# Expert routing moved into the attention loop by groups of four chunks, with a token list in DRAM (attention plus mixture of experts, one core)

## The chip, the cores and the metric

The kernel runs on one core of a Trainium2 chip. Times are device microseconds (us) of one execution. The engines of the core are PE (matrix multiply), DVE (vector), ACT (scalar), POOL (GpSimd) and SP, which here only issues transfers. Each engine works through its own list of instructions strictly in the order in which they are written, and waits on semaphores for the others. PE's clock has two levels, 1.2 and 2.4 GHz; the profile shows the granted one as 0.5 and 1.00.

## The reference, cut to what matters

```python
# x: (4, 1024, 256), 4096 tokens, 8 experts, 16 heads, chunks of 128 tokens
xn = _layernorm(x)
# attention: causal linear attention with phi(q), phi(k), then y @ w_proj.T
gate_logits = einsum('bsd,ed->bse', xn, gate_w) + gate_b + expert_bias
top_idx = argmax(gate_logits, axis=-1)
for e in range(8):
    mask = (top_idx == e)[..., None]
    h = relu(einsum('bsd,df->bsf', xn, w1[e]) + b1[e])
    y = einsum('bsf,fd->bsd', h, w2[e]) + b2[e]
    out = out + mask * y
x = x + attention(xn) + out
```

Each token goes to one expert only. The kernel sorts the tokens by expert, so that each expert's matrices meet only its own tokens.

## The kernel before

The program has two stages. The **attention loop** runs over `p` from 0 to 36. There are NC = 32 chunks of 128 tokens (`c`), and each engine works in iteration `p` on several chunks at different steps. On PE, iteration `p` holds `scores` and `st` of chunk p-3, `ktr` of p-2, `xt` of p-1 (the transpose of the normalised input, L324), `mx` in every fourth iteration, `yt1` of p-4, `inter` of p-3, `mxa` in every fourth iteration, `qk` of p-1 (L341), `yt2`, `vg` of p-1 (L355, values and gate logits), `pr` and `pv`. Nothing reorders the work: the order of the calls in each engine's loop is the order of its queue.

POOL feeds PE in this loop. In each iteration it runs, in this order: `nn` (the inverse square root of the variances, 14 dependent small instructions, in every even `p`), `km` (L1092, masks q for two heads; PE's `scores` wait for it), `w_lo` (L1101, the low half of a quarter of expert weights), `xl` (L1085, the low half of the normalised input) and a second `w_lo`. PE's `xt(c)` waits for `xl(c)`. DVE's `nb` (L606, the normalised input) waits for `nn`, and ACT's `xh` (L941) for `nb`; `xl` waits for `xh`.

DVE runs `phi` (L657), two `s_mask` (L663), `y`, two more `s_mask`, `t32`, in every fourth iteration `scale` (L720 to L724, whose result PE's `vg` waits for), `nb`, `w_max` (L698), `sums`, `res` (L691), `na`, and a second `w_max`. ACT copies results out of PSUM and makes the high halves (`w_hi`, L997).

**Routing before** comes at the end. `pick` (L754 to L768) chooses the experts of chunks 0 to 30 in one go in iteration 32, and of chunk 31 in iteration 33. `counts` on PE (L458, L460), then `bases` and `ranks` on DVE find each token's place in the sorted order. After the loop DVE builds comparison tables (L853, L856) and PE multiplies them (L519), which gives `ids`: for each of NS = 39 slots of 128 tokens the row number of each token. Then the **expert stage** gathers 128 rows of `scr` for a slot (an indirect transfer from POOL, L1136), transposes them (L528), runs the two matrices of the slot's expert (L550, L564) and scatters the result to the output (L1141).

Of the kernel before, what the change touches and what calls it, by code (L numbers as in the profile page):

```python
# [14 lines left out]
NT = B * T  # L15
# [3 lines left out]
E = 8  # L19
# [10 lines left out]
C_ID, C_MASK, C_ME, C_MH, C_ONE, C_WT, C_SL, C_T, C_N = (0, 128, 256, 258, 266, 274, 282, 321, 322)  # L30

D_RST, D_P, D_ID, D_N = (0, 264, 392, 424)
# [27 lines left out]
def program(nc, x, wall, wp, gb, eb, w1, b1, w2, b2, cst, cst2, tri, out):  # L60
    ctx = ExitStack()
    with ctx:
# [15 lines left out]
        L = sb("L", [128, NC, E], F32)  # L78
        GBE = sb("GBE", [128, 2, E], F32)
# [62 lines left out]
        PMA = PS[1][:, 392:394]  # L142
        PBX = PS[7][0:8, 0:128]
# [4 lines left out]

        VA = ST[:, 0:2048]
        R1 = VA[:, 0:256].rearrange("p (c e) -> p c e", e=E)  # L150
        R2 = VA[:, 256:512].rearrange("p (c e) -> p c e", e=E)
        O32 = VA[:, 512:768].rearrange("p (c e) -> p c e", e=E)

        TT = VA[:, 768:1032].rearrange("p (e c) -> p e c", e=E)
        PI = VA[:, 1032:1296].rearrange("p (e c) -> p e c", e=E)
        M1 = VA[:, 1296:1328]
        M2 = VA[:, 1328:1360]
        SLI = VA[:, 1360:1392].bitcast(I32)
        PLI = VA[:, 1392:1424].bitcast(I32)
        POSI = VA[:, 1424:1456].bitcast(I32)  # L160
        NSI = VA[:, 1456:1464].bitcast(I32)
        NSF = VA[:, 1464:1472]
        CSF = VA[:, 1472:1480]
        BAS = VA[:, 1480:1488]
        O16 = VA[:, 1488:1616].bitcast(BF16)
        O16C = O16.rearrange("p (c e) -> p c e", e=E)
        LC = VA[:, 1624:2048]
        EQS = VA[:, 0:624].bitcast(F16).rearrange("p (c s) -> p c s", c=32)
        WAF = WA[:, :, :, :].rearrange("p l k n -> p (l k n)")
        BO = WAF[:, 0:1248].rearrange("p (c s) -> p c s", c=32)  # L170
        GE = WAF[:, 1248:1248 + 14 * NS].bitcast(F32).rearrange("p (s e) -> p s e", e=7)
        ESF, IDZ, IDP = (WAF[:, o:o + 2 * NS].bitcast(F32) for o in (1800, 1880, 1960))
        AO = [t[:, :].bitcast(F16).rearrange("p (c n) -> p c n", c=8) for t in XR[0:4]]
# [14 lines left out]
        scr = nc.dram_tensor("scr", [NT, 512], F32, kind="Internal").ap()  # L188
        outr = out.rearrange("b t d -> (b t) d")
# [27 lines left out]

        def experts(engine, tile, unit, s):
# [10 lines left out]
        d_wall, d_wp, d_cst, d_tri, d_small, d_cst2, d_b2 = (  # L229
            sem(n) for n in ("d_wall", "d_wp", "d_cst", "d_tri", "d_small", "d_cst2", "d_b2"))  # L230
# [9 lines left out]
        names = ("sums", "na", "nn", "nb", "xh", "xl", "xt", "xTc", "qk", "relu", "exp", "phi", "km", "sc", "pv", "ktr", "kt",  # L240
# [8 lines left out]
        v_o16, t_cnt, v_es, v_bo, v_ao, t_ids, v_ids, p_xg0 = (  # L249
            sem(n) for n in ("v_o16", "t_cnt", "v_es", "v_bo", "v_ao", "t_ids", "v_ids", "p_xg0"))  # L250
# [7 lines left out]
        def sync(e):  # L258
# [27 lines left out]
            e.dma_start(WPF, wp).then_inc(d_wp, 16)  # L286
            for c in range(4, R):
                load_x(c)
            for n in range(4):
                load_split(n)  # L290
            for p in range(NC + 5):
# [12 lines left out]
                if p == NC:  # L304
                    e.wait_ge(v_wmx, NW)
                    e.dma_start(LC, cst2).then_inc(d_cst2, 16)
            e.dma_start(B2, b2).then_inc(d_b2, 16)

        def tensor(e):
# [35 lines left out]
            def vg(c):  # L345
                if c >= 1:
                    e.wait_ge(S["lg"], c)
                    e.wait_ge(S["vh"], c)
                if (c + 1) // 4 >= 1:
                    e.wait_ge(v_sc, 3 * ((c + 1) // 4))  # L350
                n = 0
# [856 lines left out]
```

## Time and profile before

| | |
|---|---|
| median of 3 runs | 545.98 us (545.52 to 548.12) |
| the profiled execution | 550.78 us |
| its span, first to last instruction | 549.0 us |
| attention loop | to about 294 us |
| routing, first gathers | 294 to 312 us |
| expert stage | 312 us to the end |
| PE busy | 484.5 us (88%) |
| DVE, ACT, POOL busy | 405.8, 280.1, 287.8 us |

The profiled execution is 0.9% longer than the median; a difference found in it is carried over to the median as it is. In a row of a timeline the first number is the start in us from the span's start, the second the duration; a bracket at its end gives the idle time before it and what ended it. Several instructions of one kind can be merged in one row (x24).

### The profile page before, as it was taken

What the parts mean: (1) busy time and instruction counts of PE and PEld (TensorE: products, weight loads), DVE (VectorE), ACT (ScalarE), POOL (GpSimd) and SP (SyncE); (2) the same over time, 40 slices, a digit from 0 to 9 for tenths busy, and PEclk for the clock granted to TensorE, in tenths of its full rate; (3) what the DMA queues carried; (4) which work ended last, traced back from release to release, by engine and by line L of the source; (5) the groups of instructions that cost most, each with busy time, mean ns of one, the idle gap of its engine ahead of it and who ended that gap; (6) DMA issues with size and microseconds to landing.
All of it is one profiled execution on the core that took longest, in us unless ns stands there. A gap on an engine that the chain in (4) does not pass through costs nothing.

```text
span 549.0 us, 17451 instructions
## 1 busy us (share of the span) xinstructions
PE 484.5 (88%) x6065; PEld 394.8 (72%) x6065; DVE 405.8 (74%) x869; ACT 280.1 (51%) x535; POOL 287.8 (52%) x480
## 2 busy tenths in 40 slices
PE   4499999999999999999862499899989989989991
PEld 1378888788878888888741388688868868868871
DVE  2768898888988898888777477677757667676671
ACT  0446878878787878878652033233323333333330
POOL 3645788777777877777434323433432433433321
PEclk9579999999999999999995599999999999999997
DMA  8322655665566556653332212222121221120100
GB/s 283 120 79 70 211 156 193 184 206 182 163 194 192 177 164 213 199 151 132 116 113 100 76 31 69 60 64 79 55 62 59 70 73 59 60 78 22 32 6 0
DMA packets 34016, 62.44 MB, mean 114 GB/s; under 512 B 5517, under 2 KB 9998, under 8 KB 33808
## 3 DMA queue, kind: packets, MB, share of 16 engines
q1 hardware_dynamic: 28944, 48.74, 28.4%
q0 software_dynamic: 4992, 12.60, 7.7%
q8 instruction: 55, 0.90, 0.6%
q14 instruction: 25, 0.20, 0.1%
HBM read 50.57 MB, written 13.50 MB: 117 GB/s over the span
## 4 chain that ended last, share of the span: by engine, by line
PE 80%; DVE 10%; issue 5%; ACT 2%; DMA 1%; POOL 1%; DVEq 0%; POOLq 0%; ACTq 0%
PE ps L550 20%; PE ps L564 19%; PE ps L341 6%; PE ps L379 6%; PE ps L408 6%; PE ps L449 6%; PE ps L355 4%; PE ps L392 3%; PE ps L422 2%; DVE AR L663 2%; PE ps L435 2%; PE ps L528 2%; PE ps L362 1%; PE ps L441 1%; PE ps L314 1%
## 5 line engine op out<-in xcount | busy, mean ns | idle before, releaser
L550 PEld LDWEIGHTS ps<-AR,W 128*128 x1872 | 131.7, 99 | 39.9 <-issue 1.0
L564 PE MATMUL ps<-W,ST 128*128 x624 | 150.8, 326 | 7.0 <-DVE AR L918 3.7
L550 PE MATMUL ps<-AR,W 128*128 128x128 f16 x1872 | 155.8, 221 | 0.8 <-ACT AR L1034 0.8
L1141 POOL DMA_INDIRECT out<-AR x39 | 39.6, 1016 | 130.0 <-DVE AR L918 130.0
L886 DVE SCALAR_TENSOR_TENSOR ST<-ps,TAs,B1S 128x512 f32<-128x512 f32 x78 | 58.5, 750 | 57.6 <-PE ps L550 56.9
L1043 ACT ACTIVATE ST<-ST 128x512 f16<-128x512 f32 x78 | 49.3, 631 | 99.9 <-DVE ST L886 96.4
L663 DVE TENSOR_TENSOR AR<-ps,CT 128x512 f32<-128x512 f32 x128 | 82.1, 684 | 12.1 <-PE ps L379 11.6
L1101 POOL TENSOR_TENSOR W<-ST,W 128x512 f16<-128x512 f32 x64 | 74.5, 1165 | 26.6 <-ACT W L997 26.2
L1092 POOL TENSOR_SCALAR AR<-AR,CT 128x256 f32<-128x256 f32 x64 | 58.7, 927 | 15.2 <-DVE AR L657 15.2
L898 DVE SCALAR_TENSOR_TENSOR ST<-ST 128x512 f16<-128x512 f32 x78 | 53.8, 690 | 15.7 <-ACT ST L1043 15.7
L1136 POOL DMA_INDIRECT AR<-scr,AR x39 | 45.4, 1165 | 28.6 <-issue 11.0
L1034 ACT ACTIVATE AR<-ps 128x512 f16<-128x512 f16 x39 | 23.3, 597 | 68.9 <-PE ps L528 68.6
L341 PE MATMUL ps<-xT,WA 128*128 128x128 f16 x768 | 50.7, 225 | 3.9 <-ACT xT L947 3.9
L564 PEld LDWEIGHTS ps<-W,ST 128*128 128x128 f16 x624 | 45.6, 98 | 10.0 <-issue 7.7
L341 PEld LDWEIGHTS ps<-xT,WA 128*128 128x128 f16 x768 | 46.7, 101 | 5.5 <-ACT xT L947 5.2
L1005 ACT ACTIVATE ST<-ST,SC 128x512 f32<-128x512 f32 x64 | 46.4, 725 | 0.0
L698 DVE TENSOR_REDUCE MX<-ST 128x1 f32<-128x512 f32 x64 | 42.5, 665 | 0.0
L997 ACT ACTIVATE W<-ST 128x512 f16<-128x512 f32 x64 | 40.4, 632 | 1.1
L379 PE MATMUL ps<-AR 32*128 32x256 f32 x512 | 37.4, 407 | 0.0
L1085 POOL TENSOR_TENSOR XR<-AR,XR 128x256 f16<-128x256 f32 x32 | 22.9, 714 | 27.3 <-ACT XR L941 27.2
L449 PE MATMUL ps<-AR 128*128 128x256 f32 x128 | 35.5, 401 | 1.4 <-ACT AR L990 1.4
L408 PE MATMUL ps<-AR 128*32 128x128 f32 x1024 | 34.6, 276 | 0.0
(144 smaller groups left out, 756.2 us busy)
## 6 DMA issues: line engine op xcount, KB each, us to landing
ST<-in_w SPq DMA_DIRECT2D x128, 256.0 KB, 4.3
scr<-XR SPq DMA_DIRECT2D x32, 256.0 KB, 2.1
XR<-in_x SPq DMA_DIRECT2D x32, 128.0 KB, 4.7
AR<-in_b SPq DMA_DIRECT2D x1, 1024.0 KB, 4.9
AR<-in_wall SPq DMA_DIRECT2D x1, 776.0 KB, 4.5
AR<-scr,AR POOLq DMA_INDIRECT x39, 3.5
out<-AR POOLq DMA_INDIRECT x39
AR<-in_wp SPq DMA_DIRECT2D x1, 256.0 KB, 4.8
```

Source lines behind the costliest of these rows:

```text
L341: a = e.matmul(PS[0][:, j * 128:(j + 1) * 128], WA[:, wl, k, j * 128:(j + 1) * 128], x_part(c, xl_, k), start=(n == 1), stop=(n == 6))
L379: a = e.matmul(PSC[r][:, g * 256:(g + 1) * 256], QK[c % 2][rows, 256 + g * 128:384 + g * 128], QM[c % 2][rows, g], start=True, stop=True)
L408: a = e.matmul(PS[5][32 * b:32 * b + 32, j * 128:(j + 1) * 128], V32[c % 2][:, 8 * g + 4 * i + b, :], S32[2 * i + t][:, (2 * g + o) * 128: ...
L449: a = e.matmul(PS[2][:, 256:512], YT2[:, k * 128:(k + 1) * 128], WPF[:, k, :], start=(k == 0), stop=(k == 1))
L550: a = e.matmul(dst, W[:, off:off + 57472][:, bass.ds(at[s], 128)], XT16[s % 2][:, xl * 256 + k * 128:xl * 256 + (k + 1) * 128], start=(n = ...
L564: a = e.matmul(PS[4 + s % 2][:, 0:w], src[h % 4][:, fs], W[:, off:off + 57344 + w][:, bass.ds(at[s], w)], start=(f == 0 and w == 512), sto ...
L663: e.tensor_tensor(S32[r].rearrange("p (b n) -> p b n", b=4), PSC[r][:, :].rearrange("p (b n) -> p b n", b=4), msk, ALU.mult).then_inc(s_[r ...
L886: e.scalar_tensor_tensor(H32[h % 2].rearrange("p (f n) -> p f n", f=4), PS[h % 4][:, :].rearrange("p (f n) -> p f n", f=4), TAs[:, :, 0][: ...
L898: e.scalar_tensor_tensor(HL2[h % 4], H32[h % 2], 0.0, HH[h % 4], ALU.max, ALU.subtract).then_inc(v_hl, 1)
L1043: e.activation(HH[h % 4], H32[h % 2], ACT.Relu).then_inc(a_hh, 1)
L1092: a = e.tensor_scalar(QM[c % 2][:, :, o, :], QK[c % 2][:, 0:256].rearrange("p (g n) -> p g n", g=2), cc(C_ME + o, 1), None, ALU.mult)
L1101: e.tensor_tensor(lo_, src, hi, ALU.subtract).then_inc(p_wlo, 1)
```

## The change

The choice of experts, the ranks and the places in the list are worked out for four chunks at a time inside the attention loop. With g as the number of the group:

- `pick` (DVE, p = 5 + 4g) takes the four chunks' logits and now has 6 instructions of 128x32 elements; the two biases are added up once beforehand.
- `ahead` (POOL, p = 5 + 4g): four dependent additions of 128x8 elements that count the tokens of the chunks ahead.
- `place` (PE, p = 6 + 4g): three matmuls of 32 columns give each token its rank within its expert plus 4096 times the expert. `own` (DVE, two small instructions) selects it, `rows` (POOL) converts it to integers.
- `put` (POOL, one for each chunk, from p = 6 on; the last four all in iteration 34): an indirect transfer that writes 128 token numbers of 4 bytes each to their places in the list `lst` in DRAM. `lst` is filled with an out-of-range number at the start.
- `slots` (DVE, p = 34) works out which 39 rows of the list hold tokens. One indirect transfer on POOL reads these 39 rows of 128 numbers into `TOK`, PE transposes them, and DVE copies them to `ids`.
- The comparison tables, their 32 matmuls and a constant's load in the loop are gone.

Beside this: POOL's `km` is halved, ACT makes the other half (`km`, after `xTc`). ACT runs `xh` and the second `w_hi` after `relu` and `exp` instead of before. On DVE `scale` moves from behind the last two `s_mask` and `t32` to behind `y`. POOL clears the gather buffers in iteration 35, ahead of the last four `w_lo`, instead of behind them.

```diff
+            def place(p):
+                g = group(p, 6)
...
+                e.wait_ge(v_o16, g + 1)
+                e.wait_ge(p_ox, g + 1)
...
+                e.matmul(PRK, tri16[:, :], O16[:, g % 2], start=True, stop=False)
+                e.matmul(PRK, one16[:, :], OX[:, g % 2], start=False, stop=False)
+                a = e.matmul(PRK, one16[0:1, :], B4[:, :, :], start=False, stop=True)
...
+            def pick(p):
+                g = group(p, 5)
...
+                e.tensor_tensor(R1[:, :, :], l, bm(GBE[:, 2, :], 4), ALU.add).then_inc(dv.up(), 1)
...
+                e.tensor_tensor(o, bc(M1[:, :], E), w, ALU.is_equal).then_inc(v_o16, 1)
...
+                own(p)
                 if on(p - 4):
                     y(p - 4)
+                scale(p)
                 if on(p - 3):
                     s_mask(p - 3, 2)
                     s_mask(p - 3, 3)
                     t32(p - 3)
-                scale(p)
                 if on(p) and p > 0:
                     nb(p)
                 w_max(2 * p)
+                pick(p)
...
-            e.tensor_tensor(BO, EQS, bc(LC[:, D_ID:D_ID + 32], NS), ALU.mult).then_inc(v_bo, 1)
-            for g in range(4):
-                e.wait_ge(d_scr[g], 16 * (NC // R))
-                e.tensor_tensor(AO[g], bm(LC[:, D_P:D_P + 128], 8), bc(M2[:, 8 * g:8 * g + 8], 128),
-                                ALU.is_equal).then_inc(v_ao, 1)
...
+            def ahead(p):
...
+                e.wait_ge(v_o16, g + 1)
...
+                for i in range(4):
+                    dst = OX[:, g % 2, i + 1] if i < 3 else OX[:, (g + 1) % 2, 0]
+                    a = e.tensor_tensor(dst, OX[:, g % 2, i], O16[:, g % 2, i], ALU.add)
...
+            def put(c):
...
+                e.indirect_dma_start(lst, bass.IndirectOffsetOnAxis(POS[:, c % 4:c % 4 + 1], 0),
+                                     cc(C_TK + c, 1), None, bounds_check=E * NT - 1,
+                                     oob_is_err=False).then_inc(d_put[c % 4], 16)
...
                 if on(p - 2):
-                    km(p - 2)
+                    km2(p - 2)
+                ahead(p)
+                rows(p)
+                if p < NC + 2:
+                    if on(p - 6):
+                        put(p - 6)
+                elif p == NC + 2:
+                    for c in range(NC - 4, NC):
+                        put(c)
+                if p == NC + 3:
+                    e.wait_ge(S["pv"], NC)
+                    for i in range(NG):
+                        e.memset(XG[i], 0.0).then_inc(p_xg0, 1)
                 w_lo(2 * (p - 5))
                 if on(p):
                     xl(p)
                 w_lo(2 * (p - 5) + 1)
+                if p == NC + 2:
+                    e.wait_ge(v_row, 1)
+                    for i in range(4):
+                        e.wait_ge(d_put[i], 16 * (NC // 4))
+                    e.indirect_dma_start(TOK, None, lst.rearrange("(r n) o -> r (n o)", n=128),
+                                         bass.IndirectOffsetOnAxis(ROI[0:NS, :], 0), bounds_check=E * NT // 128 - 1,
+                                         oob_is_err=False).then_inc(d_tok, 16)
```

The queue of POOL in an iteration p = 9 (a second group's `pick`) and the start of the next, before: one masking pair (L1092), `w_lo`, `xl`, `w_lo`, then `nn` of p = 10.

```order
L1092 TENSOR_SCALAR AR<-AR,CT 128x2x128 [waits s_sc,s_phi]
L1092 TENSOR_SCALAR AR<-AR,CT 128x2x128
L1101 TENSOR_TENSOR W<-ST,W 128x512 [waits a_whi]
L1085 TENSOR_TENSOR XR<-AR,XR 128x256 [waits s_xh]
L1101 TENSOR_TENSOR W<-ST,W 128x512 [waits a_whi]
L1063 TENSOR_SCALAR rsn<-mv 128x2 [waits s_nb,s_na]
```

The same place after. L1106 is the half of the masking that is left, L1119 `ahead`, L1141 a `put`, L1150 `w_lo`, L1100 `xl`.

```order
L1106 TENSOR_SCALAR AR<-AR,CT 128x2x128 [waits s_sc,s_phi]
L1119 TENSOR_TENSOR OX<-OX,O 128x8 [waits t_rk,v_o16]
L1119 TENSOR_TENSOR OX<-OX,O 128x8 [waits po] x3
L1141 DMA lst<-CT,POS 32768x1
L1150 TENSOR_TENSOR W<-ST,W 128x512 [waits a_whi]
L1100 TENSOR_TENSOR XR<-AR,XR 128x256 [waits s_xh]
L1150 TENSOR_TENSOR W<-ST,W 128x512 [waits a_whi]
L1078 TENSOR_SCALAR rsn<-mv 128x2 [waits s_nb,s_na]
```

One masking instruction has gone; four additions that wait for DVE's `pick` (v_o16) and one indirect transfer now stand ahead of `w_lo` and `xl`.

DVE in such an iteration after, from the end of `pick` on (L775 to L788), with `sums` (L609), `res` (L710) and `phi` (L676) behind it:

```order
L775 TENSOR_TENSOR R<-L,GBE 128x32 [waits s_lg]
L777 TENSOR_REDUCE M<-R 128x4 [waits dv]
L779 TENSOR_TENSOR R<-R,M 128x32 [waits dv]
L781 TENSOR_TENSOR R<-R,CT 128x32 [waits dv]
L783 TENSOR_REDUCE M<-R 128x4 [waits dv]
L788 TENSOR_TENSOR O<-M,CT 128x32 [waits dv]
L609 BN_STATS st<-XR 128x6 [waits s_na,d_x3]
L710 TENSOR_TENSOR XR<-ps,XR 128x256 [waits s_pr]
L616 BN_AGGR mv<-st 128x2 [waits s_nn,s_sums]
L717 TENSOR_REDUCE MX<-ST 128x1 [waits d_wm3]
L676 SCALAR_TENSOR_TENSOR AR<-ps,AR 128x512 [waits s_exp]
```

Before, `sums` followed the first `w_max` at once; now six dependent instructions stand between them.

POOL at the end of the attention loop before, the last four iterations' `w_lo` (L1101), the clearing of the gather buffers (L1126) and the first gathers (L1136):

```order
L1101 TENSOR_TENSOR W<-ST,W 128x512 [waits a_whi] x4
L1101 TENSOR_TENSOR W<-ST,W 128x2x256 [waits a_whi] x4
L1126 MEMSET AR 128x512 [waits s_pv]
L1126 MEMSET AR 128x512 x3
```

And after, from the last `ahead` to the first gather (L1205); L1134 is `rows`, L1192 the reading of the list:

```order
L1119 TENSOR_TENSOR OX<-OX,O 128x8 [waits po] x3
L1141 DMA lst<-CT,POS 32768x1
L1150 TENSOR_TENSOR W<-ST,W 128x512 [waits a_whi] x2
L1134 CAST POS<-M 128x4 [waits d_put2,d_put1,d_put3,d_put0,v_pos]
L1141 DMA lst<-CT,POS 32768x1 [waits p_pos]
L1141 DMA lst<-CT,POS 32768x1 x3
L1150 TENSOR_TENSOR W<-ST,W 128x512 [waits a_whi] x2
L1192 DMA ST<-lst,ST 39x128 [waits d_put2,d_put1,d_put3,d_put0,v_row]
L1183 MEMSET AR 128x512 [waits s_pv]
L1183 MEMSET AR 128x512 x3
L1150 TENSOR_TENSOR W<-ST,W 128x2x256 [waits a_whi] x4
L1205 DMA AR<-scr,AR 128x512 [waits d_scr4,d_scr5,d_scr3,d_scr6,d_scr2,d_scr7,d_scr1,v_ids,d_scr0,p_xg0]
```

Six indirect transfers now stand in POOL's queue between the last `ahead` and the first gather.

## Rows read from the trace of the kernel before

**Rows 1.** Engines' busy time by stretches: columns PE, PEld, DVE, ACT, POOL, clock, DMA

```profile
166.00:197.50 31.50, 31.25 (x431) 26.69 (x427) 27.34 (x66) 25.43 (x53) 24.48 (x49) 1.00 0.58 183
...
294.00:312.00 18.00, 2.38 (x36) 1.67 (x36) 13.25 (x30) 0.33 (x2) 6.79 (x10) 0.50 0.31 102
```

**Rows 2.** Timeline of PE, xt of two chunks, and PE's wait for scale

```profile
183.12 0.39 PE L324 MATMUL ps<-id,XR 128*128 128x128 f16 x4
...
190.82 0.39 PE L324 MATMUL ps<-id,XR 128*128 128x128 f16 x4
...
PE ps L355 <- DVE SC L724: 1.9, 7, 0.3
```

**Rows 3.** Timeline of DVE, sums in an iteration p = 4n + 1; nb's durations

```profile
179.59 0.42 DVE L593 BATCH_NORM_STATS2 st<-XR 128x6 f32<-128x256 f32 x1
...
L606 DVE TENSOR_SCALAR AR<-XR,mv,rsn x32: 404/408/1424, 15.1 to 257.2; 128x256 f32<-128x256 f32 x32
```

**Rows 4.** Timeline of DVE: pick of 31 chunks and of one

```profile
267.81 0.41 DVE L754 TENSOR_TENSOR ST<-L,GBE 128x248 f32<-128x248 f32 x1
268.25 0.42 DVE L756 TENSOR_TENSOR ST<-ST,GBE 128x248 f32<-128x248 f32 x1
...
277.68 0.16 DVE L754 TENSOR_TENSOR ST<-L,GBE 128x8 f32<-128x8 f32 x1
277.87 0.17 DVE L756 TENSOR_TENSOR ST<-ST,GBE 128x8 f32<-128x8 f32 x1
```

**Rows 5.** Timeline of POOL, iteration p = 4n + 2 from nn on

```profile
181.49 0.22 POOL L1063 TENSOR_SCALAR rsn<-mv 128x2 f32<-128x2 f32 x1
...
184.85 0.19 POOL L1074 TENSOR_SCALAR nr<-nr 128x2 f32<-128x2 f32 x1
185.13 0.20 POOL L1076 TENSOR_TENSOR rsn<-rsn,nr 128x2 f32<-128x2 f32 x1
185.30 1.84 POOL L1092 TENSOR_SCALAR AR<-AR,CT 128x256 f32<-128x256 f32 x2
187.11 1.16 POOL L1101 TENSOR_TENSOR W<-ST,W 128x512 f16<-128x512 f32 x1
188.23 0.67 POOL L1085 TENSOR_TENSOR XR<-AR,XR 128x256 f16<-128x256 f32 x1
188.86 1.16 POOL L1101 TENSOR_TENSOR W<-ST,W 128x512 f16<-128x512 f32 x1
```

**Rows 6.** Gathers by line (ns, least/median/most; idle us, times), then the last scatter's chain

```profile
L1136 POOL DMA_INDIRECT AR<-scr,AR x39: 997/1029/1548, 307.5 to 518.9; - x39
  issue: 11.0, 36
...
539.19 0.73 issue
539.92 0.98 POOL out L1141
```

**Rows 7.** Timeline of PE at the end of attention, and the clock behind

```profile
271.88 0.53 PE L362 MATMUL ps<-CT,AR 128*128 128x128 f32 x2 [1.72 <-DVE AR L657]
...
284.88 0.28 PE L458 MATMUL ps<-ST,tri 128*128 128x256 bf16 x1
285.00 0.27 PE L460 MATMUL ps<-ST,one 128*128 128x256 bf16 x1
...
272.00:274.00 2.00, 1.88 (x9) 1.58 (x10) 1.34 (x4) 1.52 (x4) 2.00 (x3) 0.52 0.00 0
```

**Rows 8.** Timeline of DVE and POOL between the stages

```profile
271.15 0.68 DVE L657 SCALAR_TENSOR_TENSOR AR<-ps,AR 128x512 f32<-128x512 f32 x1
...
300.51 4.62 DVE L856 TENSOR_TENSOR XR<-ST 128x1024 f16<-128x1024 f32 x4
...
295.40 1.95 POOL L1126 MEMSET AR<- 128x512 f32 x4
...
307.53 1.27 POOL L1136 DMA_INDIRECT AR<-scr,AR  x1 [10.18 <-DVE AR L867]
```

More of the change, by code:

```diff
@@ L149, in program @@
         VA = ST[:, 0:2048]
[L150 to L173, printed above, removed]
+        NSI = VA[:, 0:8].bitcast(I32)
+        NSF, CSF, DOF, GEP = (VA[:, 8 * i:8 * i + 8] for i in range(1, 5))
+        ROW = VA[:, 40:41]
+        ROI = VA[:, 41:42].bitcast(I32)
+        ESF = VA[:, 64:64 + NS]
+        GE = VA[:, 128:128 + 7 * NS].rearrange("p (s e) -> p s e", e=7)
+        TOK = VA[0:NS, 512:640]
         wt = cc(C_WT, 8)
@@ L188, in program @@
         scr = nc.dram_tensor("scr", [NT, 512], F32, kind="Internal").ap()
+        lst = nc.dram_tensor("lst", [E * NT, 1], F32, kind="Internal").ap()
         outr = out.rearrange("b t d -> (b t) d")
@@ L216, in weights, with group @@
             return src.rearrange("p (f n) -> p f n", f=2), w[:, :, 0], w[:, :, 1]
+        def group(p, first):
+            g = (p - first) // 4
+            return g if (p - first) % 4 == 0 and 0 <= g < NC // 4 else None
         def experts(engine, tile, unit, s):
@@ L350, in vg @@
                     e.wait_ge(v_sc, 3 * ((c + 1) // 4))
+                if group(c + 1, 6) is not None:
+                    e.wait_ge(v_pos, group(c + 1, 6) + 1)
                 n = 0
@@ L490, in tensor @@
                 mx(p)
+                place(p)
                 if p == 2:
@@ new lines, in pick, with own @@
+                e.tensor_tensor(o, bc(M1[:, :], E), w, ALU.is_equal).then_inc(v_o16, 1)
+            def own(p):
+                g = group(p, 6)
+                if g is None:
+                    return
+                e.wait_ge(t_rk, g + 1)
+                e.tensor_tensor(R1[:, :, :], PRK, O16[:, g % 2], ALU.mult).then_inc(dv.up(), 1)
+                e.wait_ge(dv.sem, dv.n)
+                if g >= 1:
+                    e.wait_ge(p_pos, g)
+                e.tensor_reduce(M2[:, :], R1[:, :, :], X_AX, ALU.add).then_inc(v_pos, 1)
@@ L966, in kt, with km @@
                 e.activation(KT32[c % 2], PS[0][:, 0:256], ACT.Copy).then_inc(S["kt"], 1)
+            def km(c):
+                e.wait_ge(S["phi"], c + 1)
+                if c >= 2:
+                    e.wait_ge(S["sc"], c - 1)
+                e.activation(QM[c % 2][:, :, 0, :], QK[c % 2][:, 0:256].rearrange("p (g n) -> p g n", g=2),
+                             ACT.Copy, scale=cc(C_ME, 1)).then_inc(S["km"], 1)
             def vh(c):
@@ L977, in lg @@
             def lg(c):
-                e.activation(L[:, c, :], PS[1][:, 256:264], ACT.Copy, scale=sv(1)).then_inc(S["lg"], 1)
+                if c >= 8:
+                    e.wait_ge(v_o16, c // 4 - 1)
+                e.activation(L[:, c // 4 % 2, c % 4, :], PS[1][:, 256:264], ACT.Copy, scale=sv(1)).then_inc(S["lg"], 1)
             def y1(c):
```

226 lines of the change are left out of this document (115 added, 111 removed).

## The prediction

> **What bounds the kernel now.** I read the busy time by stretches first. In four iterations of the attention loop PE is busy for 31.25 of 31.50 us, while DVE has 4.1 us free and POOL 7.0 us, some of it only short gaps between dependent instructions [rows 1]. PE sets the pace: one `xt` follows the other after 7.70 us [rows 2]. The one thing that PE waits for regularly is DVE's `scale`, 1.9 us in 7 waits [rows 2]. Between 294 and 312 us PE has 2.38 us of work and waits for the routing at half clock [rows 1]. So there are two accounts: what the change saves at the seam of the stages, and what it puts in the way of a PE that has no slack in the loop. In the loop nothing PE does can be late for free, so the question for each added step is only whether it reaches PE.
>
> **Account 1, the seam.** Before, the first gather is at 307.53 [rows 8]. What stands before it and goes: `pick` of 31 chunks holds DVE from 267.81 to 271.15, 3.34 us, and the next `phi` with it, for which PE waits 1.72 us [rows 4, 7, 8]; the tables, of which the last four instructions alone take 4.62 us [rows 8]. What will stand there instead is POOL's queue; I follow it in the time frame of before, without the delays from account 2.
> - The last `pick`: that of one chunk started at 277.68 [rows 4]. Without the 3.34 us, and since `pick` now stands ahead of `res`, which costs it about 1.1 us less waiting (an estimate from the order alone), it starts at 273.2.
> - Its six instructions are of 32 elements. Start to start it is 0.19 us at 8 elements and 0.44 at 248 [rows 4]; at 32 that is 0.22, so 1.35 us for six. POOL sees it 0.1 us later.
> - `ahead`: dependent small instructions on POOL follow at 0.28 us [rows 5]: 3 x 0.28 + 0.20 = 1.05 us. To 275.7.
> - An indirect transfer holds POOL for 1.03 us, plus 11.0/36 = 0.31 us ahead of it in a stream [rows 6]: **1.31 us**. With the gap of an isolated one, 0.73 us, it is 1.73 us [rows 6]. The trace has no transfer of 4-byte elements; these two are my bounds. It has the same 128 addresses as a gather, and compute instructions stand ahead of it that let POOL prepare, so I take the lower.
> - From 275.7: one `put` 1.31, two `w_lo` at 1.16 [rows 5], `rows` 0.3 (one small instruction and a wait), four `put` 5.25, two `w_lo`, the reading of the list 1.31, clearing 1.95 [rows 8], four `w_lo` 4.64. That gives 295.1, and the first gather some 0.3 us later, 295.4. The gain is **12.1 us**; with 1.73 us for each of the six transfers and 0.73 at the gather it is 9.2.
> - What could bind later than POOL: the list lands some 3 us after 288.5, is transposed and copied by about 292.5; the last rows of `scr` are written by about 292. Both are before 295.
>
> **Account 2, the loop.** `scale` moves ahead of two `s_mask`: PE's 1.9 us of waits go (**-1.9**). `place` adds three matmuls with their own weights; the two of this kind before were issued 0.12 us apart [rows 7], so 0.3 us for each group and all of it on PE, since PE has no gap. ACT's half of `km` and the later `xh` I cost at nothing: ACT has 6 us free in 31.5 [rows 1], and POOL's `xl`, which waits for `xh`, has to be ready more than a us later than `xh` will be in the iterations without `pick`.
>
> The expensive part is the order on POOL. `ahead` waits for `pick` of the same iteration, and `put`, `w_lo` and `xl(p)` stand behind it; PE's `xt(p)` waits for that `xl`. The iteration around 180 us is one in which `pick` will be:
> - `pick` can start where `sums` starts now, at 179.59 [rows 3]. DVE is there tied to PE's progress through `y`, so it can't come earlier.
> - From there: pick 1.35, semaphore 0.1, `ahead` 1.05, `put` 1.31, `w_lo` 1.12, `xl` 0.67 [rows 4 to 6], 5.6 us. `xl` is ready at 185.2. PE wants it at 183.12 [rows 2]. PE waits **2.1 us** (2.5 with the dearer transfer).
> - The next iteration starts from that late `xl`. POOL runs `w_lo` to `nn`'s start 1.2 us, `nn` 3.81 (181.49 to 185.30), half of `km` 0.92, `rows` 0.3, `put` 1.31, `w_lo` 1.12, `xl` 0.67 [rows 5, 6]: 9.35 us from one `xl` to the next. PE needs 7.70 + 0.3 = 8.0 us from one `xt` to the next. PE waits another **1.35 us** (1.8).
> - In the third iteration there is no `nn` and POOL catches up (5.2 us of work for 7.7). In the fourth `nn` is back, but it starts early enough: from the second `xl` on, two iterations of work come to 14.7 us against 15.9 on PE. Then POOL idles until the next `pick`. So the delay does not grow, and it comes back in each group.
>
> For each group 2.1 + 1.35 + 0.3 = 3.75 us (4.65 with the dearer transfer). Groups 1 to 6 have all of it, 22.5 us (27.9). Group 0 has no `put` yet in its first iteration, 0.8 + 1.35 + 0.3 = 2.45 us (3.0). Group 7 lies in account 1. At the start POOL gets two more small instructions ahead of the second `xl`, 0.4 us.
>
> **The sum**: -12.1 - 1.9 + 22.5 + 2.45 + 0.4 = **+11.4 us**; with the dearer transfer -9.2 - 1.9 + 27.9 + 3.0 + 0.4 = +20.2 us. Against the profiled execution's 550.78 us this is 562.2; against the median of 545.98, 0.9% lower, it is **557.4 us**, 2.1% slower.
>
> **POOL and DVE sharing a path.** `nb` took 408 ns at the median and 1424 ns once [rows 3], and one gather took 1548 ns where most took 1029 [rows 6]: now and then an instruction of one of the two waits for the other. If each of the 13 `put` on PE's path met such a case, 0.5 us each, the sum would be 6.5 us more. I don't count it, since 1 in 39 gathers can hardly be told from the median. The Trainium skill, SBUF — State Buffer, sections SBUF: two separate sides and Who interferes with whom, says that a DVE instruction in a two-port mode takes the path shared with GpSimd for its whole length and that the other blocks, and it names descriptor writing as a victim. By that rule a `put` would wait for at most one `nb`. The trace agrees only in part: `nb` mostly ran at 408 ns beside a busy POOL.
>
> **The rivals.**
> - *A `put` hardly holds POOL* (the engine goes on while the descriptors are written). This one ends faster. With 0.3 us instead of 1.31, the two waits fall to 1.1 and 0.35 us, a group to 1.75: 10.5 + 1.45 - 1.9 + 0.4 = +10.5 in the loop. The seam then is bound by the list and the last `scr` rows at about 293, gain 14.5. Sum -4, **542 us**. Against it: the gathers stand 1.3 us apart with nothing else in the queue. For it: POOL's spans are rough, and the gathers show the spacing of transfers alone, not that of a compute instruction behind one. Each 0.1 us of a `put` is worth 1.9 us (13 in the loop, 6 at the seam), so the sign turns at 0.7 us. Chance 0.15.
> - *The late `xl` does not reach PE*, because DVE gets ahead of its present place after the first wait, or `pick` is quicker. Then -12.1 - 1.9 + 2.1 + 0.4 = -11.5, **534.5 us**. Against it: `y` waits for `yt1` of the same iteration, and the distance from there to `pick` is a sum of DVE durations. Chance 0.07.
> - *Half of it*: cheaper transfers and one of the two waits. 543 to 549 us, chance 0.12.
> - *PE's clock falls in the waits.* After 1.72 us of waiting PE's granted clock was 0.52 from 272 to 274 us [rows 7]; the waits forecast here are 2.1 us long and come seven times. At half clock PE falls back by about 1.7 us each time, but the second wait of a group, for POOL, takes up 1.35 of that. So it adds 0.4 to 1.7 us a group, and with the dearer transfer this gives 564 to 573 us. Chance 0.16.
> - The forecast: 551 to 564 us, chance 0.50.
>
> **How the numbers follow.** A measurement of this kernel can tell about 0.5% (2.7 us) from no change. Faster by more: the first two rivals, which give 0.22. Within 0.5%: most of the third, 0.10. Slower: 0.68. The range for 8 in 10 leaves out the second rival, part of the first and the dearest ends of the fourth: 540 to 569 us. The likeliest case by itself has 551 to 564.
>
> **What would show it.** In the profile after: POOL's four additions wait for DVE's `pick` in every fourth iteration, some 4 us in all; PE's transposes (L331) have a wait of about 2 us for POOL's `xl` (L1100) in one iteration and 1 to 1.5 us in the next, six times each; four iterations take 35 us where they took 31.5. The waits for `scale` are gone. The first gather comes 12 us after the place it would have in a loop without delays, so near 319 us, and the expert stage is as long as before. The prediction is wrong if a `put` holds POOL for less than 0.7 us, if `pick` starts earlier relative to PE's `yt1`, or if the clock falls in most groups.

## The result, and the profile after

The changed kernel takes **578.17 us** (576.65 to 579.97, 4 runs) against 545.86 us (545.52 to 548.12, 4 runs) on the same chip, a ratio of 1.058 (95% interval 1.054 to 1.063). Slower was forecast; the size was not: 557.4 us, with 569 as the upper end. The runs of the kernel before fall into two groups, 545.4 to 546.6 and 548.0 to 551.2 us, whose mix changes from one set of runs to the next (its median by sets: 545.9 to 549.3), so two ratios from different sets can differ by up to 0.6% for that alone. The traces show where in the program such a difference can arise: PE's clock is at half level until 33 us in the profiled execution of before, and only in part of that stretch in the one of e4, whose loop is as long.

```profile
20.00:33.00 13.00, 11.31 (x81) 9.24 (x85) 7.28 (x18) 5.90 (x13) 7.08 (x23) 0.50 0.40 122
...
20.00:33.00 13.00, 10.60 (x118) 8.70 (x116) 9.47 (x23) 6.30 (x15) 7.72 (x20) 0.85 0.35 107
```

The first row is of before, the second of e4. The sixth `xt` stands at 56.87 us in the one and at 52.27 in the other; in after it stands at 57.35.

The profiled execution of after took 579.97 us, 17.8 us more than the 562.2 that the prediction's sum gives for the profiled execution. The rows below say where these 17.8 us are. Busy time by stretches, with the columns of [rows 1]:

```profile
166.00:202.00 36.00, 31.67 (x426) 26.30 (x425) 29.32 (x75) 26.60 (x58) 26.21 (x54) 1.00 0.69 165
...
294.00:338.00 44.00, 18.15 (x199) 12.69 (x196) 18.06 (x55) 16.03 (x30) 23.07 (x29) 0.73 0.47 95
```

PE now has 4.3 us free in four iterations of 36 us, where it had 0.25 in 31.5 [rows 1]. Its clock is at 1.00 in this stretch. The share of DMA has risen from 0.58 to 0.69, though the rate fell from 183 to 165 GB/s: the transfers have become longer, not more. The waits from 60 to 300 us (engine, line, waited for; sum, times, longest):

```profile
POOL OX L1119 <- DVE O L788: 27.3, 6, 4.8
...
PE ps L331 <- POOL XR L1100: 15.5, 11, 2.1
...
DVE AR L622 <- POOL rsn L1091: 9.5, 7, 1.7
...
PE ps L389 <- DVE XR L710: 6.9, 14, 0.8
...
ACT ST L1017 <- DMA ST<-in_w: 2.3, 5, 0.7
```

The first two rows are the forecast: `ahead` waits for `pick`, and PE's `xt` for `xl`. The other three were not forecast: DVE's `nb` (L622) waits for POOL's `nn`, PE's `scores` (L389) for DVE's `res` (L710), and ACT's scaling of weights for their load. In PE's timeline the waits for `xl` and for `res` stand in each group; here are the second iteration of one and the first two of the next:

```profile
208.06 1.15 PE L389 MATMUL ps<-AR 32*128 32x256 f32 x16 [0.77 <-DVE XR L710]
...
210.85 0.40 PE L331 MATMUL ps<-id,XR 128*128 128x128 f16 x4 [0.76 <-POOL XR L1100]
...
233.14 1.15 PE L389 MATMUL ps<-AR 32*128 32x256 f32 x16 [0.37 <-DVE XR L710]
...
236.86 0.40 PE L331 MATMUL ps<-id,XR 128*128 128x128 f16 x4 [2.12 <-POOL XR L1100]
...
243.84 1.15 PE L389 MATMUL ps<-AR 32*128 32x256 f32 x16 [0.77 <-DVE XR L710]
...
246.63 0.40 PE L331 MATMUL ps<-id,XR 128*128 128x128 f16 x4 [0.76 <-POOL XR L1100]
...
252.57 1.15 PE L389 MATMUL ps<-AR 32*128 32x256 f32 x16 [0.17 <-DVE XR L710]
```

`xt` waits 2.12 us in one iteration (forecast 2.1; 1.70 in some groups) and 0.76 in the next (forecast 1.35); the 0.77 for `scores` ahead of it makes up the rest and 0.18 more. The waits of 0.37 and 0.17 for `res` stand beside the forecast ones. POOL in the first of these iterations:

```profile
232.41 1.03 POOL L1119 TENSOR_TENSOR OX<-OX,O 128x8 bf16<-128x8 bf16 x4 [4.36 <-DVE O L788]
233.95 1.04 POOL L1141 DMA_INDIRECT lst<-CT,POS  x1 [0.50 <-issue]
235.02 1.16 POOL L1150 TENSOR_TENSOR W<-ST,W 128x512 f16<-128x512 f32 x1
236.14 0.67 POOL L1100 TENSOR_TENSOR XR<-AR,XR 128x256 f16<-128x256 f32 x1
```

A `put` holds POOL for 1.04 us. Ahead of it stand 0.50 us behind `ahead`, 0.3 in a stream, and 0.78 behind `rows`, whose result it waits for: 1.3 to 1.8 us, where 1.31 was taken and 1.73 was the upper bound. So the price of the step that was in doubt was nearly right, a little low behind `rows`. Now POOL at the seam, from the last `ahead` to the first gather:

```profile
302.90 1.04 POOL L1119 TENSOR_TENSOR OX<-OX,O 128x8 bf16<-128x8 bf16 x4 [4.60 <-DVE O L788]
304.45 1.04 POOL L1141 DMA_INDIRECT lst<-CT,POS  x1 [0.51 <-issue]
305.52 2.28 POOL L1150 TENSOR_TENSOR W<-ST,W 128x512 f16<-128x512 f32 x2
309.28 0.19 POOL L1134 CAST POS<-M 128x4 int32<-128x4 f32 x1 [1.48 <-DMA lst<-CT,POS]
310.24 1.00 POOL L1141 DMA_INDIRECT lst<-CT,POS  x1 [0.77 <-POOL POS L1134]
...
314.13 0.98 POOL L1141 DMA_INDIRECT lst<-CT,POS  x1 [0.31 <-issue]
315.12 2.28 POOL L1150 TENSOR_TENSOR W<-ST,W 128x512 f16<-128x512 f32 x2
326.45 1.01 POOL L1192 DMA_INDIRECT ST<-lst,ST  x1 [9.05 <-DMA lst<-CT,POS]
...
333.99 1.06 POOL L1205 DMA_INDIRECT AR<-scr,AR  x1 [0.16 <-issue]
```

Two waits for puts to land, 1.48 and 9.05 us, stand in POOL's queue. The durations between them are close to the forecast ones. How long one put takes from issue to landing:

```profile
DMA to landing us min/median/max: 3.9/6.3/11.4
```

The longest is that of the last one; it stands in the chain that ended last:

```profile
314.13 11.36 DMA lst<-CT,POS
```

**The 17.8 us.** The last instruction of the last `pick` should have started at 273.2 + 5 x 0.22 = 274.3 in the frame without delays, plus 23.5 us of delay in the loop, 297.8; it started at 302.63. The loop thus cost 4.8 us more than forecast, as far as the estimated start of `pick` without delays is right. From there to the first gather the prediction had 21.1 us; it took 31.4, 10.3 more, and the two waits are 10.5. After the last scatter's issue (566.43) the span runs 11.67 us on, before it was 549.0 - 539.92 = 9.08 [rows 6]: 2.6 more. Together 17.7. The expert stage itself, from the first gather to the last scatter, is as long as before: 232.4 us in both. Against the forecast median of 557.4 us the miss is 20.8 us, 3.0 more: the prediction took 4.8 us off its profiled figure to get to the median, and after's profiled execution lies only 1.8 us above its median.

### The profile page after: what moved, and what is told of

Same layout as the page of the kernel before. It is cut to its first block, busy times and chain, and to the rows that moved or that the text cites. A ratio compares the mean times of both kernels' runs of the same rounds, so it can differ in the third digit from the quotient of the medians.

```text
span 578.1 us, 17672 instructions
## 1 busy us (share of the span) xinstructions
PE 487.2 (84%) x6057; PEld 396.6 (69%) x6057; DVE 404.7 (70%) x902; ACT 288.0 (50%) x567; POOL 296.6 (51%) x524
## 4 chain that ended last, share of the span: by engine, by line
PE 62%; POOL 14%; DVE 9%; issue 8%; DMA 4%; ACT 1%; POOLq 0%; DVEq 0%; ACTq 0%
PE ps L566 18%; PE ps L580 18%; PE ps L348 4%; PE ps L389 3%; POOL W L1150 3%; DMA lst<-CT,POS 3%; PE ps L418 3%; PE ps L402 3%; POOL lst L1141 2%; PE ps L459 2%; PE ps L445 2%; PE ps L432 2%; PE ps L364 2%; POOL XR L1100 2%; PE ps L544 2%
## 5 line engine op out<-in xcount | busy, mean ns | idle before, releaser
L1150 POOL TENSOR_TENSOR W<-ST,W 128x512 f16<-128x512 f32 x64 | 74.3, 1165 | 4.2 <-ACT W L1009 3.4
L1205 POOL DMA_INDIRECT AR<-scr,AR x39 | 40.6, 1041 | 19.1 <-issue 11.2
L389 PE MATMUL ps<-AR 32*128 32x256 f32 x512 | 36.8, 399 | 9.1 <-DVE XR L710 7.2
L1141 POOL DMA_INDIRECT lst<-CT,POS x32 | 33.8, 1056 | 13.2 <-issue 6.9
L389 PEld LDWEIGHTS ps<-AR 32*128 32x128 f32 x512 | 24.3, 184 | 16.5 <-issue 16.3
## 6 DMA issues: line engine op xcount, KB each, us to landing
AR<-in_b SPq DMA_DIRECT2D x1, 1024.0 KB, 12.7
```

Source lines behind the costliest of these rows:

```text
L389: a = e.matmul(PSC[r][:, g * 256:(g + 1) * 256], QK[c % 2][rows, 256 + g * 128:384 + g * 128], QM[c % 2][rows, g], start=True, stop=True)
L1150: e.tensor_tensor(lo_, src, hi, ALU.subtract).then_inc(p_wlo, 1)
```

## The experiments

Ratios are to the kernel before on the same chip, with 95% intervals; "after" is 1.058. e2, e3, e5, e6, e7 and e9 do not compute the reference: their list lacks the tokens whose puts are left out or go elsewhere (e3 lacks three chunks, e2, e5, e6 and e7 all but the last four, e9 all), and the expert stage moves no rows for these. In the traces of e2, e5, e6, e7 and e9 that stage takes 231.0 to 231.1 us instead of 232.4, so some 0.3% of their gain is this. "The loop" below is the time from the sixth `xt` to the last: 204.8 us in before, 232.8 in after.

| run | what | ratio | interval |
|---|---|---|---|
| e1 | `ahead` behind `xl` | 1.034 | 1.030 to 1.038 |
| e2 | no puts in the loop | 1.020 | 1.017 to 1.023 |
| e3 | one last put, not four | 1.047 | 1.045 to 1.050 |
| e4 | before, `scale` early | 0.999 | 0.997 to 1.001 |
| e5 | e1 and e2 | 1.011 | 1.007 to 1.015 |
| e6 | e1, puts of 512 bytes | 1.019 | 1.015 to 1.023 |
| e7 | e1, puts 512 bytes apart | 1.019 | 1.015 to 1.024 |
| e8 | before, all side edits | 1.009 | 1.006 to 1.012 |
| e9 | e7, the last four too | 1.002 | 0.999 to 1.004 |
| e10 | a complete list of that kind | 1.006 | 1.004 to 1.009 |
| e11 | e10, `xh` early on ACT | 1.017 | 1.010 to 1.024 |
| e12 | e10, seam reordered | 1.002 | 0.999 to 1.004 |
| e13 | before, side edits without late `xh` | 1.002 | 0.999 to 1.006 |
| e14 | e12, `slots` split | **0.994** | 0.992 to 0.996 |

**The place of `ahead` (e1).**

```diff
-                ahead(p)
                 rows(p)
...
                 if on(p):
                     xl(p)
+                ahead(p)
```

> Changed kernel with one move on POOL: the four additions of ahead stand behind xl instead of ahead of put, w_lo and xl. Nothing else is changed. Theory A (what costs in the loop is that xl stands behind a wait for pick): by the time xl is done pick has ended, so ahead no longer waits long; four iterations fall from 35.8 us to 31.5 to 32.5 us, PE's waits for xl (L1100) nearly go, and the time falls by 20 to 25 us, to 553 to 558 us. Theory B (POOL simply has too much to do with the puts, wherever the wait stands): four iterations stay above 34.5 us, and the time stays above 570 us. The seam between the stages is the same in both.

568.45 us, between the ranges of both theories. The wait of `xt` for `xl` nearly goes, and another comes out (60 to 260 us):

```profile
ACT ST L1017 <- DMA ST<-in_w: 12.3, 5, 3.6
...
PE ps L331 <- POOL XR L1100: 2.7, 4, 0.8
```

The order on POOL is worth 2.4% by the ratios; the medians, from two chips, differ by 9.7 us and the traced spans by 12.7, of which 9.8 are in the loop. What it uncovers are weight loads that land late. A put took 7.3 us to land here, a weight load 5.9 (4.3 before).

**The puts themselves (e2, e5).** The call of `put` in the loop is left out.

> Changed kernel without the 28 indirect transfers of the loop (puts of chunks 0 to 27); the last four stay. The list in DRAM then holds only the last 512 tokens, so most slots gather and scatter nothing. Theory A (the puts are 1.1 to 1.5 us each in the two iterations in which xl is late): each group loses 2.5 to 3 us, four iterations fall to about 33 us and the loop is 15 to 18 us shorter. Theory C (the wait for pick by itself is the cost, the puts hardly matter): four iterations stay above 35 us. The landing of the last put tells something as well: if it stays near 11 us after its issue, earlier puts have no part in it.

560.88 us. The loop takes 218.4 us, 14.4 less than in after, four iterations 33.6: Theory A, roughly. Even without these puts the kernel is 2.0% slower: `ahead` still waits for `pick` ahead of `xl`. And the last put landed 14.3 us after its issue, with POOL's reading of the list waiting behind it:

```profile
311.13 1.00 POOL L1188 DMA_INDIRECT ST<-lst,ST  x1 [11.94 <-DMA lst<-CT,POS]
```

So the puts of the loop have no part in the late landing of the last four. Both edits together:

> Both earlier edits together: ahead stands behind xl, and the loop's 28 puts are left out (the list then holds only the last 512 tokens). Theory F (the loop's excess has two parts, the place of ahead and the puts, and nothing else): four iterations take 31.5 to 32.2 us as in the kernel before, and the weight loads land in 4.3 us. Against e2, whose loop took 33.6 us for four iterations, that is 8 to 12 us less in all: 549 to 553 us where before is 549. Rival: ACT's new half of km, the later xh and place cost PE by themselves, then four iterations stay above 32.7 us.

552.87 us, in the expected range, but with 32.6 us for four iterations (31.5 before, 35.8 after), between what Theory F and its rival expected: the place of `ahead` and the puts are not quite all of the loop's excess.

**Size or address (e6, e7).** Both have e1's order and write the loop's puts into a second tensor. The first added line is of e6, the others are of e7.

```diff
+                dst, val = (lst2, cc(C_ID, 128)) if c < NC - 4 else (lst, cc(C_TK + c, 1))
...
+                e.tensor_scalar(POS[:, :], M2[:, :], 128.0 if g < NC // 4 - 1 else 1.0, None,
+                                ALU.mult).then_inc(p_pos, 1)
```

> As e1 (ahead behind xl), but the loop's 28 puts write 512 bytes for each token into a tensor of 512-byte rows instead of 4 bytes into the list (the list then holds only the last 512 tokens). In e1 a put landed 7.3 us after its issue and the weight loads in 5.9 us. Theory G (writes of a few bytes are slow by themselves and hold the transfer engines): with 128 times the bytes the puts land in 2 to 4 us, as the scatters of the expert stage do, the weight loads are back at 4.2 to 4.6 us, and the time falls to 551 to 556 us. Rival H (any 128 scattered writes from POOL's queue beside the loads do it): landings stay near 7 us and the time near 565 us.

> As e1, but the loop's 28 puts write their 4 bytes at places 512 bytes apart in another tensor (the list then holds only the last 512 tokens). In the list, tokens of one expert stand at neighbouring addresses, so several transfer engines write into the same few bytes' neighbourhood. Theory I (neighbourhood is what makes them slow): the puts land in 2 to 4 us and the weight loads in 4.2 to 4.6 us, as forecast for e6. Theory G (the size alone): as slow as in e1, landing near 7 us, weight loads near 5.9 us, time 565 to 569 us.

558.26 and 559.10 us, both 1.5% below e1, of which 0.3% is the shorter expert stage. The landings are as Theories G and I have them, the times are above their 551 to 556 us. The queue's issues in e7 (KB each, median us to landing), which in after read 5.1, 3.2 and 6.3:

```profile
ST<-in_w SPq DMA_DIRECT2D x128, 256.0 KB, 4.1
scr<-XR SPq DMA_DIRECT2D x32, 256.0 KB, 2.2
...
lst<-CT,POS POOLq DMA_INDIRECT x32, 3.7
```

Words of 4 bytes that lie 512 bytes apart land as fast as rows of 512 bytes (3.7 us in both), those next to each other take twice that (7.3 in e1). So it is the neighbouring address and not the small size; that it isn't the second tensor either, e10 shows below. The Trainium skill, DMA: Bandwidth & Descriptors, section Specifications, says that transfers under 512 bytes are done as read-modify-write. Taken as a rule on size it would make e7 as slow as e1; the trace shows that it isn't.

**The last four puts (e3, e9).**

> Changed kernel with one put instead of four in iteration 34 (chunks 28 to 30 are left out of the list; their tokens get no expert). Theory D (the writes of several puts are worked off one after the other, some 3.5 us each): the single put lands 4 to 5 us after its issue as in the loop, the reading of the list starts 10 to 11 us earlier, and the time falls by 8 to 11 us. Theory E (the landing is slow because of the weight loads and b2 beside it, whatever the number of puts): the landing stays near 10 us, and the time falls only by the 3.9 us of the three issues, or less.

575.37 us.

```profile
319.48 1.00 POOL L1191 DMA_INDIRECT ST<-lst,ST  x1 [3.10 <-DMA lst<-CT,POS]
```

POOL's wait before the reading of the list was 3.10 us instead of 9.05, so the single put had landed 6.4 us after its issue at the latest. From the last `pick` to the first gather it took 8.9 us less, 3.9 of them the three issues. That is nearer to Theory D, but the whole gained only 1.1% (2.8 us by the medians): in the traces the loop, whose code is the same as in after, took 236.1 us instead of 232.8. Loops with such puts differ by 3 us from one trace to another, and no run here shows why.

> As e7 (ahead behind xl, puts 512 bytes apart in a second tensor), but now the last four puts are spread as well, so the list that is read stays empty and the expert stage moves no token rows. Theory D+I (the last four puts of neighbouring addresses land one after the other, 3 to 4 us apart, and hold up the weight loads beside them, and that is why the seam gained nothing): the reading of the list waits some 3 us for the puts instead of 9.6, the time falls 6 to 8 us below e7, ratio 1.004 to 1.009. Rival (the puts land late because the queue or the weight loads are full then, not because of their addresses): the wait stays at 8 us or more, and the ratio at 1.017 to 1.021.

548.62 us, and the reading follows at once (in e7 it waits 9.61 us for puts):

```profile
296.67 1.01 POOL L1194 DMA_INDIRECT ST<-lst,ST  x1 [0.20 <-issue]
```

That is 1.8% below e7, somewhat more than expected, and from the last `xt` to the first gather the traces differ by 8.6 us. The rival (the queue is full then anyway) has fallen.

**The side edits (e4, e8, e13).**

> Kernel before with scale moved ahead of the last two s_mask and t32 on DVE, nothing else. Expected: PE's seven waits for scale, 1.9 us, go, and the time falls by 1.5 to 3.5 us, to 542.5 to 544.5 us. Rival: the s_mask that are now later hold pv instead, and nothing changes.

549.62 us, no change. The waits for `scale` (1.9 us in 7, [rows 2]) went, and a wait of the same sum took their place:

```profile
PE ps L379 <- DVE XR L691: 2.0, 6, 0.4
```

PE's `scores` now wait for `res`, which stands behind `scale`'s former place: what DVE does in an iteration stays the same, and PE meets it at the next step.

> Kernel before with all edits beside the routing: scale moved ahead of the last two s_mask, half of km on ACT, xh and the second w_hi behind relu and exp. The routing is that of before. My prediction costed these at -1.9 us (scale) and nothing (the rest). e4 showed that scale alone gives no measurable gain. Expected: the same as before within 0.5%, 547 to 551 us. Rival: POOL's relief by 0.9 us an iteration shortens the loop, 3 us or more less.

552.27 us, 0.9% slower: not free. The traces have 2.0 us of it in the loop (206.8 us against 204.8); where the rest of the 4.3 us between the medians lies they don't show, their spans differ by 1.3 only. To tell the parts apart:

> The kernel before with scale moved early and half of km on ACT; ACT's xh and w_hi stay where they were ahead of relu and exp. e8 had the later xh as well and was 0.9% slower. If the half of km on ACT costs (it stands ahead of w_hi, relu and exp): ratio 1.005 to 1.012, as e8. If the later xh costs (xl, res and PE's scores wait): 0.997 to 1.003.

549.55 us, ratio 1.002 (0.999 to 1.006), with 204.9 us for the loop. So the 2.0 us in the loop are the later `xh`, not the half of `km`, and most of the 0.9% is likely to be as well. But the sign depends on the loop around it:

> As e10, with ACT's xh and second w_hi back in their place ahead of relu and exp. If the order on ACT is what made e8 0.9% slower (a later xh makes xl, nn's neighbours and res late): 3 to 5 us less than e10, ratio 0.997 to 1.008. If it was the half of km on ACT instead: the same as e10 within 0.3%.

558.93 us: with the early `xh` it is 1.1% *slower* than e10, the version described below, which has the late one. Its loop takes 6.7 us more. Neither expectation for e11 was met. In its trace ACT waits 16.7 us in 17 places for `nb` with `relu` and `exp` queued behind, and PE's `scores` wait 9.2 us for `res` (3.2 in e10); in e10 ACT has no such wait. So where `xh` should stand depends on how late `nb` is, and with puts in the loop it is late.

**A list with spread addresses (e10, e12, e14).** These compute the whole reference. The word for rank r of an expert goes to 256 (r mod 128) + its row, so neighbours in rank lie 1024 bytes apart, in a list as long as before; `own` makes the address, one transfer in SP's queue reads the list, PE transposes it, and two matmuls with a 0/1 table pick the 39 slots.

```diff
+                e.scalar_tensor_tensor(POS[:, g % 2], MI[:, 1], 256.0, MI[:, 2], ALU.mult,
+                                       ALU.add).then_inc(v_pos, 1)
...
+            e.dma_start(COL, lst.rearrange("(p n) o -> p (n o)", p=128)).then_inc(d_tok, 16)
...
+            for k in range(2):
+                a = e.matmul(PSL, LT[:, 128 * k:128 * k + 128], SEL[:, NS * k:NS * k + NS],
+                             start=(k == 0), stop=(k == 1))
```

> A complete version: ahead behind xl, and the list laid out so that consecutive ranks of an expert lie 1024 bytes apart; own makes the addresses in four more small DVE instructions, rows on POOL is gone, the list is read by one plain transfer of 128 KB in SP's queue, transposed on PE, and two matmuls with a 0/1 table pick the 39 slots. Theory I: puts land in about 3.7 us, in_w in 4.1, period of four iterations 33 to 33.5 us as in e7, and at the seam no wait of 9 us; some 2 us of added work there. Time 550 to 556 us, ratio 1.005 to 1.015. Rival (the gain of e7 came from writing to another tensor than the one that is read, or from anything but the distance): the loop as in e1, ratio 1.03 or more.

551.87 us, as expected. A put lands in 2.4 us though it goes into the list that is read, so the rival of e7 (another tensor) has fallen. Four iterations take 32.1 us, and POOL no longer waits for puts. But the first gather is only at 305.36. PE waits 6.8 us for the last `y`, because `slots` stands ahead of it on DVE, and the list's reading had been put behind a wait for the last `w_lo`.

```diff
-                if p == NC + 2:
-                    slots()
...
+                if p == NC + 3:
+                    slots()
...
+                if c == NC - 1:
...
+                    e.dma_start(COL, lst.rearrange("(p n) o -> p (n o)", p=128)).then_inc(d_tok, 16)
...
+                if s == 0:
+                    w_lo(NW - 2)
+                    w_lo(NW - 1)
```

> As e10, with the seam reordered: slots (all but its first instruction) behind the last y on DVE instead of ahead of it, the list read ahead of the last scr write in SP's queue and without the wait for the last w_lo, the last two w_lo behind the first gather. In e10 PE waits 7 us for the last y (two of slots' instructions take 2.9 and 2.0 us while POOL works beside them), and the list is read at 299.7 although the puts had landed by about 290. If the seam's order is what still costs: first gather at 295 to 298 instead of 305.4, ratio 0.986 to 0.996, faster than before. Rival (the instructions of slots are slowed wherever they stand, or POOL's own queue of w_lo and clearing holds the first gather): first gather at 301 or later, ratio 0.999 to 1.005.

548.02 us, first gather at 301.86: 3.5 us earlier where 7 to 10 were expected, and with that in the range of the rival. ACT's copy ahead of the last `y` came 2.6 us late (the core's records don't show what held it), and `res` of the last chunk stood behind `slots`, 2.2 us after PE's last `pr` was done. So `slots` was cut in two:

> As e12, but the first part of slots (up to the products that stand in front of the row sums) stays ahead of the last y, where POOL is issuing puts and DVE is idle, and only the five small instructions behind them stand after the last y. In e12 slots took from 292.6 to 298.2 us behind the last y, with two instructions slowed beside POOL's clearing and w_lo, so that res of chunk 31 started 2.2 us after PE had its input, and ACT's copy ahead of the last y started 2.6 us late for a reason outside of the core. If what is left of the seam is DVE's order: first gather at 296 to 299 instead of 301.9, ratio 0.990 to 0.998. Rival (the late copy on ACT comes again, or the list is what comes last): first gather at 300 to 302, ratio 0.999 to 1.003.

**544.70 us** (544.07 to 546.01, 12 runs; before on that chip 548.45, 545.52 to 550.92, 17 runs): ratio 0.994, the only version below the kernel before. The gain is small: e12 and e13 were measured against 23 other runs of before on the same chip, with a median of 546.02 us, and by these e14 would be at 0.998. In the traces, whose sixth `xt` stand alike at 56.83 and 56.87 us, e14's span is 543.0 us and that of before 549.0. Its seam, PE, DVE and POOL together:

```profile
289.75 2.07 PE L469 MATMUL ps<-AR 128*128 128x256 f32 x4 [0.47 <-ACT AR L1037]
...
290.21 1.93 POOL L1205 MEMSET AR<- 128x512 f32 x4
...
290.38 4.01 DVE L854 TENSOR_SCALAR ST<-ST,CT 128x39 f32<-128x39 f32 x1
...
292.09 2.26 POOL L1174 TENSOR_TENSOR W<-ST,W 128x512 f16<-128x512 f32 x2
...
294.61 0.42 DVE L729 TENSOR_TENSOR XR<-ps,XR 128x256 f32<-128x256 f32 x1
...
298.36 1.06 POOL L1223 DMA_INDIRECT AR<-scr,AR  x1 [4.01 <-DMA scr<-XR]
```

An instruction of 39 columns (L854) took 4.01 us, until 294.39, when POOL's clearing and two `w_lo` were done (294.35); the same one took 0.24 us in e12, where POOL was idle. PE's last `pr` was done at 291.82, so `res` (L729) is 2.8 us late, and the gather waits for its row in `scr`. Whether that can be gained wasn't tried.

## Why the prediction was wrong

**What was right.** PE sets the pace and has no slack; the order on POOL (`pick`, `ahead`, `put`, `w_lo`, `xl`) is the largest cost, with the wait of 2.12 us where 2.1 was worked out. The price of a put on POOL, on which the sign hung, was right within its two bounds, but for the 1.8 us behind `rows`. (By the prediction's own figures the lower bound is 1.03 + 0.31 = 1.34 us and not 1.31, some 0.6 us over all puts on the path.) The first three rivals, a cheap put, a hidden `xl` and half of it, didn't occur.

**The fourth rival, the falling clock, did occur, in two groups of the loop, and cost next to nothing.** The granted clock fell to 0.50 behind waits of 1.70 us for `xl` that ended at 129.29 and 272.65, and was back at 1.00 before the next `xt`; it did not fall behind a wait of 1.70 that ended at 201.08, nor behind those of 2.12. The means of the two stretches:

```profile
129.00:134.00 5.00, 4.71 (x42) 4.58 (x43) 2.78 (x8) 2.39 (x5) 3.91 (x15) 0.66 0.68 85
...
273.00:277.00 4.00, 4.00 (x33) 3.89 (x31) 2.77 (x8) 2.39 (x5) 3.01 (x13) 0.57 0.76 68
```

The next `xt` came 9.77 and 9.76 us later, as in the groups without a fall (9.77 from the `xt` at 236.86 to the next, above): the wait for POOL in the second iteration took all of it up, not only the 1.35 us that the prediction allowed for. So its 0.4 to 1.7 us a group are not part of the miss.

**The step that failed: the sum lets POOL read the list directly behind the last puts and two `w_lo`, with the landing of the puts at nothing.** In the prediction's queue from 275.7 there is `rows` at 0.3, four `put` at 5.25, two `w_lo`, and then "the reading of the list 1.31"; both `rows` and the reading wait for puts to land (the order of POOL's queue after names d_put0 to d_put3 at L1134 and L1192), and no term stands for that. Nor does it come under "What could bind later than POOL", where only the landing of the reading itself is bounded, at "some 3 us" taken from no row (it was 4.8 us, and POOL's queue behind it was longer). The four last puts landed 4.4 to 11.4 us after their issues, about 3.6 us apart, and the two waits took 10.5 us, nearly all of the gain of 12.1. Without them the time would have come out near 568 us, just inside the forecast range (an estimate: 578.17 less 10.5). e9 takes the late landing away: from the last `xt` to the first gather it needs 8.6 us less than e7, and the ratio is 1.8% lower. e2 and e3 show that the last four make each other late: they do so without any put in the loop, and one alone lands within 6.4 us.

**Loop: the mechanism right, the size too small, +4.8 us.** Four iterations take 35.8 us on average, where the prediction's terms give 35.25 (31.5 + 3.75). Of the 28.0 us by which after's loop is longer than that of before, the order of `ahead` has 9.8 (after, e1), neighbouring addresses 7.8 (e1, e7), puts at distant addresses 3.5 (e7, e5), and 6.9 are left in e5. For these 6.9 the prediction had `place` at 0.3 us a group; e8 has 2.0 us for the side edits in the loop of before, and the rest isn't told apart. The puts make the weight loads and the writes of `scr` slower (5.1 and 3.2 us to land, against 4.3 and 2.1 before). How much that costs in the order of after, where `xl` is what PE waits for, wasn't measured by itself. The `scores` wait for `res`, 6.9 us in 14 waits, which the two waits worked out for each group had only in part. With 3 us between two traces of one loop (e3), the split of the 4.8 us stays open.

**"PE's 1.9 us of waits go" and the side edits "at nothing".** e4 shows 0 where -1.9 stood, and e8, all side edits together, shows 0.9% where -1.9 us stood, 2.0 us of it in the loop. Since e11 shows that the later `xh` has the other sign in a loop with spread puts, these can't be added to the account of after, and the 4.8 us above hold whatever they came to in it.

**After the last scatter, +2.6 us.** Not in the forecast at all. From the issue of the last scatter to the end of the span: 9.08 us in the kernel before and 9.1 in e4 (78 indirect transfers), 9.4 in e2 and e5 (83), 11.46 in e3 (108), 11.67 in after (111), 11.62 in e10 (110). e2 differs from after only in the 28 puts and the waits for them: 0.08 us each. What is done in that time no row shows.

**The account in the traces**, us, one execution each:

| | to the sixth `xt` | to the last `xt` | to the first gather | to the last scatter | to the end |
|---|---|---|---|---|---|
| before | 56.9 | 204.8 | 45.9 | 232.4 | 9.1 |
| after | 57.4 | 232.8 | 43.9 | 232.4 | 11.7 |
| e1 | 57.0 | 223.0 | 41.3 | 232.5 | 11.7 |
| e7 | 58.0 | 215.2 | 41.4 | 231.0 | 11.6 |
| e9 | 57.7 | 214.5 | 32.8 | 231.1 | 11.7 |
| e5 | 56.3 | 211.6 | 42.3 | 231.1 | 9.4 |
| e14 | 56.8 | 208.9 | 32.7 | 233.0 | 11.7 |

With puts that land in time and its own order at the seam, e14 gains 13.2 us there (45.9 to 32.7), where 12.1 was forecast for after: a gain of that size was there to be had. Of it 4.1 us are lost again in the loop and 2.6 at the end.

## What to carry over

When a change adds a transfer that the trace doesn't have, bound its landing from both sides as well as the time it holds its engine, and ask what else is in flight: the forecast priced a put's issue within 0.5 us and missed 10 us behind it. Scattered small words belong at distant addresses, even if the list must then be transposed to be read. And a wait removed from the engine that sets the pace is worth nothing before the next thing it meets has been looked up: `scale` was replaced by `res` to a tenth of a us (1.9 and 2.0).

## What the runs showed that was not expected

- **Neighbouring words.** Indirect writes of 128 words of 4 bytes land in 6.3 to 7.5 us at the median (after, e1, e3; at most 14.3, in e2) when their addresses adjoin, in 2.4 to 3.7 us when they are 512 or 1024 bytes apart (e7, e9, e10), and other transfers slow down with the former: loads of 256 KB from 4.1 to 5.9 us, the writes of `scr` from 2.2 to 5.0 (e7, e1). Where in the memory path this happens stays open.
- **DVE beside POOL.** A DVE instruction of 0.24 us took 4.01 us beside POOL's clearing and two `w_lo` (e14), one of 0.17 us took 1.46 (e12). `nb`, for which [rows 3] has only one such case, 1424 ns, took 1.27 to 1.29 us in seven iterations of after, each time starting 0.04 to 0.06 us behind a `w_lo`. The Trainium skill, SBUF — State Buffer, section Who interferes with whom, says that a DVE instruction in a two-port mode and GpSimd block each other for whole instructions. The trace agrees in that `nb` ended 0.14 to 0.17 us behind the `w_lo`, and it shows more: in e14 DVE was held over two rows of POOL, six instructions that followed each other without a gap. In which mode the DVE instructions ran no row shows.
- **The end of the program** grew by 0.08 us for each indirect transfer in these kernels, as counted above.
